# A four-layer graph network kernel whose engine loops are written out

## What is computed

```python
h = jnp.maximum(_layernorm(x), 0.0)
x = x + L0(h)   # typed projections k, q, v; a = <k[src] W, q[dst]> per head; softmax over the
                # edges of a target; sum of v[src] W * attn into dst; projection, norm, FiLM
h = jnp.maximum(_layernorm(x), 0.0)
x = x + L1(h)   # segment_sum of (h * in_degree**-0.5)[src] into dst, * out_degree**-0.5
h = jnp.maximum(_layernorm(x), 0.0)
x = x + L2(h)   # gates = sigmoid(h[src] W_src + h[dst] W_dst + edge_attr W_edge);
                # segment_sum(h[src] W_msg * gates) / segment_sum(gates) + h W_root + b + h
h = jnp.maximum(_layernorm(x), 0.0)
x = x + L3(h)   # gelu(layer_norm(mean of h[src] over the edges of dst @ W_l + b_l + h @ W_r))
```

## Time and profile before

| | us |
|---|---|
| median of 3 runs | 5004.62 |
| lowest, highest | 5002.63, 5007.93 |
| span of the profiled execution | 5005.4 |
| POOL busy | 3394.4 (68%) |
| DVE busy | 3080.3 (62%) |
| PE busy | 3026.9 (60%) |
| ACT busy | 1509.9 (30%) |

### The profile page before, as it was taken

How to read it: one execution, slowest core, us unless ns; L and a number is a source line. 1 busy time by engine, 2 the same in 40 slices (tenths; PEclk the granted TensorE clock), 3 DMA queues, 4 the chain that set the end, 5 groups by cost and what they waited for, 6 DMA issues and landing times.

```text
span 5005.4 us, 77541 instructions
## 1 busy us (share of the span) xinstructions
PE 3026.9 (60%) x15687; PEld 2538.2 (51%) x15688; DVE 3080.3 (62%) x8200; ACT 1509.9 (30%) x2868; POOL 3394.4 (68%) x3564
## 2 busy tenths in 40 slices
PE   6655556555562444455555999999995444444443
PEld 4445555555562444444444777777774344444443
DVE  6567777777777666645453777777775444444443
ACT  2223333333221000011112666666663122222222
POOL 2567777777403777777774777777774777777775
PEclk9667777777775555567676999999998555555555
DMA  3467777788712222222225667767775222222224
GB/s 93 129 184 233 231 225 230 229 227 232 182 35 55 53 52 52 53 63 65 66 65 88 188 187 187 187 187 184 189 187 97 56 56 56 56 56 56 56 56 41
DMA packets 533908, 616.11 MB, mean 123 GB/s; under 512 B 95419, under 2 KB 418043, under 8 KB 533724
## 3 DMA queue, kind: packets, MB, share of 16 engines
q0 software_dynamic: 142256, 349.44, 27.5%
q1 hardware_dynamic: 391468, 264.70, 19.7%
HBM read 529.54 MB, written 84.25 MB: 123 GB/s over the span
## 4 chain that ended last, share of the span: by engine, by line
POOL 44%; issue 20%; DMA 15%; DVE 9%; PE 7%; DVEq 2%; ACT 2%; SPq 1%; POOLq 0%; ACTq 0%
POOL G L708 44%; DMA G<-tab,SRC 10%; DMA mvd<-G 3%; DVE ACCR L1426 3%; PE PB L515 2%; PE PSA L919 1%; PE PB L1106 1%; DVEq L667 1%; PE PB L508 1%; DVE ACCR L1915 1%; DMA MV<-mvd 1%; SPq L791 1%; DVE FLG L1897 1%; ACT PB L1272 0%; ACT L1143 0%
## 5 line engine op out<-in xcount | busy, mean ns | idle before, releaser
L708 POOL DMA_INDIRECT G<-tab,SRC x3520 | 3355.8, 953 | 1378.5 <-issue 1045.4
L1426 DVE TENSOR_TENSOR ACCR<-ACCR,PSA 128x128 f32 (+2 forms) x3536 | 1128.7, 319 | 740.2 <-PE PSA L919 379.9
L919 PE MATMUL PSA<-G,S 128*128 128x128 f32 x3520 | 855.8, 419 | 1159.3 <-DMA G<-tab,SRC 963.9
L919 PEld LDWEIGHTS PSA<-G,S 128*128 128x128 f32 x3520 | 734.7, 309 | 1269.4 <-DVE ACCR L1426 688.8
L1409 DVE TENSOR_TENSOR S<-PB,REL 128x512 f32<-128x512 f32 x884 | 606.5, 686 | 38.6 <-DVE MASK L1478 12.9
L1044 PE MATMUL PB<-QTR,ST 128*128 x1792 | 347.4, 355 | 308.0 <-ACT ST L1235 166.8
L1044 PEld LDWEIGHTS PB<-QTR,ST 128*128 128x128 f32 x1792 | 306.0, 257 | 344.5 <-issue 343.7
L919 PE MATMUL PSA<-FLG,S 128*128 128x256 f32 x1760 | 422.5, 383 | 4.1 <-DVE FLG L1897 3.8
L919 PEld LDWEIGHTS PSA<-FLG,S 128*128 128x128 f32 x1760 | 337.3, 192 | 150.7 <-issue 88.8
L919 PE MATMUL PSA<-SCR,S 128*128 128x137 f32 x1792 | 335.1, 345 | 16.8 <-DVE ACCR L1426 16.7
L919 PEld LDWEIGHTS PSA<-SCR,S 128*128 128x128 f32 x1792 | 311.0, 251 | 21.5 <-DVE SCR L1806 21.5
(11 more groups left out here) (321 smaller groups left out, 3700.5 us busy)
## 6 DMA issues: line engine op xcount, KB each, us to landing
mvd<-G SPq DMA_DIRECT2D x224, 256.0 KB
MV<-mvd SPq DMA_DIRECT2D x224, 256.0 KB
G<-tab,SRC POOLq DMA_INDIRECT x3520, 2.5
SCR<-in_ea_t SPq DMA_DIRECT2D x880, 64.0 KB
S<-relt SPq DMA_DIRECT2D x224, 128.0 KB, 5.1
SCR<-reld SPq DMA_DIRECT2D x220, 128.0 KB
tab<-SCR SPq DMA_DIRECT2D x57, 128.0 KB, 1.8
tab<-G SPq DMA_DIRECT2D x50, 128.0 KB, 1.7
```

The source lines that it names most:

```text
L708: nc.gpsimd.indirect_dma_start(out=rows[:, slot, j, :], out_offset=None, in_=table, in_offset=bass.IndirectOffsetOnAxis(ap=SRC[:, k:k + 1] ...
L919: last = nc.tensor.matmul((PSA if banks is None else banks)[:, par, j, 0:width], S[:, slot, j, :], rhs(j), start=True, stop=True)
L1426: v_.tensor_tensor(rows, rows, banks[:, par, j, 0:width], ALU.add).then_inc(s["rows_added"], 1)
```

## The change

Every `Fori` of the four helpers, of `sp_mixed` and of `sp_results` becomes a Python loop over the same range. The same functions are called with the same indices in the same order, but as numbers: the work instructions, their operands and their semaphores stay, wait values and addresses become constants, and the register arithmetic and branches are gone. Values that come from memory (which block a tile belongs to) are still loaded into registers (`TENSOR_LOAD` at L667 and L675). GpSimd's program is not changed. Two tests in the code change their outcome with the index being a number: `plan(b)` is called for every block, and does nothing above 19; and a wait on a value of zero or less is left out.

```diff
@@ steps
-            if sz.iters > lead + 1:
-                with eng.Fori(lead, sz.iters - 1) as i:
-                    for u in range(UNROLL):
-                        fn(i, u)
+            for i in range(lead, sz.iters - 1):
+                for u in range(UNROLL):
+                    fn(i, u)
@@ layer0_steps
-                with eng.Fori(i, j) as r:
+                for r in range(i, j):
@@ pairs
-            if n > lead + tail:
-                with eng.Fori(lead, n - tail) as i:
-                    for r in range(2):
-                        fn(i * 2 + r, r)
+            for b in range(2 * lead, NS - 2 * tail):
+                fn(b, b % 2)
@@ early_steps
-            with eng.Fori(2, calm) as i:
+            for i in range(2, calm):
...
-            with eng.Fori(first, sz.iters - 1) as i:
+            for i in range(first, sz.iters - 1):
@@ sp_mixed
-            with sp.Fori(1, TURNS_ALL // 2) as k:
-                for r in range(2):
-                    store(k * 2 + r, r)
+            for t in range(2, TURNS_ALL // 2 * 2):
+                store(t, t % 2)
@@ sp_results
-            with sp.Fori(1, TURNS_ALL) as t:
+            for t in range(1, TURNS_ALL):
```

## The result

| | us |
|---|---|
| before, median of 7 runs (range) | 5002.97 (4999.73 to 5007.93) |
| after, median of 7 runs (range) | 4987.85 (4984.73 to 4991.92) |
| ratio, 95% interval | 0.9972 (0.9961 to 0.9982) |
| span of the profiled execution, before and after | 5005.4, 4986.0 |

The change makes the kernel 0.28% faster, 14 us by the ratio, with an interval from 9 to 20. The profiled executions differ by 19.4 us, which is more than the ratio says: that of before was the slowest of its seven.

What follows compares the result with a forecast made beforehand. GpSimd's gathers were taken to bound the edge stages, leaving the second projection's loop: 12.6 + 0.4 + 0.3 = 13.3 us off the 5,004.62 us median gives 4,991.3 us, range 4,987 to 4,997 (4,984 to 5,003 with rival 1 and packets).

Steps and rivals of the forecast that it cites:

- What bounds the kernel: Edge stages: GpSimd's gathers set the rate, 4,457.7 of 5,005.4 us; other engines' edits gain only from GpSimd's waits or between stretches.
- The projection, 12.6 us: Projection behind the scores, 1,440 to 1,509 us: 21 intervals of 2.70 us become 2.10, saving 12.6 us.
- TensorE could do 1.02, VectorE's part comes to 1.05: Second projection, per block: VectorE still late next at 1.05 us, where TensorE's nine matmuls need 1.02.
- The bound of 13.9 us: Second projection: the most to be had if TensorE alone sets the pace, 21 x (2.70 - 2.04).
- Ends of 0.4 and 0.3 us: Entry of the first projection's loop saves some 0.4 us; SyncE's loop of stores at the end 0.3 us.
- Inside the stages 0: Edge stages: no gain from their loops, hidden behind gathers; longer programs also cost 0, at most 10 us.
- The sum: Whole kernel: 12.6 + 0.4 + 0.3 = 13.3 us off the median of 5,004.62, giving 4,991.3 us, 0.27% faster.
- Rival 1: Second projection: only loop control goes, about 0.33 us a turn, 7.7 us with the ends, 4,996.9 us; chance 0.11.
- Rival 2: Scores stage gives back 7 us of short waits and some 3 of gather time, 4,981 us; chance 0.08.
- Rival 3: Gathers: 190 more instruction packets delay them by 0.15 us each, costing 28 us, 5,020 us; chance 0.08.
- Rival 4: Second projection: TensorE's clock stays at 0.50, 30 us more, 5,034 us; chance 0.03.
- The rule on the taken branch: Old loops: a skill's rule that far taken branches stall would speak for more than 12.6 us; no row showed it.

Runs made afterwards that it cites:

- e2: The whole change against the kernel before, except that the projections' helper `pairs` keeps its loop; ratio 1.0002, median 4999.61 us.
- e3: The kernel before with the projections' helper `pairs` written out on VectorE alone; ratio 0.9975, two blocks 2.20 us.
- e4: The kernel before with `pairs` written out on TensorE, ScalarE and SyncE but not on VectorE; ratio 0.9993, two blocks 2.62 us.
- e1: The kernel before with only the projections' helper `pairs` written out, all other loops kept; ratio 0.9971, two blocks 2.12 us.
- e7: The changed kernel with VectorE's residual add of the second projection one block later; ratio 0.9964 against before, two blocks 2.00 us.
- e9: The changed kernel with an empty two-turn loop on VectorE before each even block of the second projection; ratio 0.9993 against before, two blocks 2.38 us.
- e5: The kernel before with four blocks a turn in the second projection's loop, register waits kept; ratio 0.9985, two blocks 2.27 or 2.70 us.
- e6: The kernel before with each pair of blocks in `pairs` a loop of one turn; ratio 0.9970, two blocks 2.12 us.
- e8: The changed kernel with 40 more ScalarE semaphore increments per step in turns 2 to 25 of the last edge stage; ratio 0.9983 against before.

## Why the prediction was right, and where not

**What bounds the kernel: right.** The stages stayed at GpSimd's rate. e2 is the proof: all edge loops gone, ratio 1.0002 (0.9993 to 1.0011).

**The projection, 12.6 us: right in place, engine and about in size.** A turn went from 2.70 to 2.12 us, where I had 2.10: 21 x 0.58 = 12.2. e3 and e4 confirm that VectorE was the engine, but for 0.08 of the 0.58, which belong to TensorE's loop; e1 and e2 show that no other loop counts. The mean seam is 228.1 us in the three kernels with all loops in the pairs (229.1, 227.5, 227.8) and 215.9 in those five above: 12.2 us.

**"TensorE could do 1.02, VectorE's part comes to 1.05": wrong in its reading.** The 1.05 of the last two blocks was no engine's own time. In before VectorE does a block in 0.92 us where it waits for nothing, from its L555 at 1503.07 to this one:

```profile
1503.99 0.55 DVE L555 TENSOR_TENSOR G<-ACCR 128x384 f32 x1
```

And 1.05 is every second interval of TensorE, in the loop and behind it, whatever the other one is: 1.65 over a jump, 1.22 from 1504.81 to 1506.03 in the earlier trace rows, which was not counted. Two blocks of that end take 2.27 us; that twice 1.05 came so close to the 2.12 of the change was in part luck. VectorE's work and TensorE's work both fit in 1.00 (e7). The two waited for each other over the order of VectorE's instructions, and one block of delay for the add removes it. The bound of 13.9 us, from 1.02, was therefore too low: 21 x (2.70 - 2.00) = 14.7. The 0.113 us for one more matmul came from two group rows whose ends are modelled.

**Ends of 0.4 and 0.3 us: not to be seen one by one.** The first gather comes at 173.9 us in the mean of the five kernels that loop over the first projection on VectorE (174.7, 173.2, 174.1, 173.2, 174.3) and at 173.1 in the mean of the seven that have it written out on all engines. That is of the order of 0.4 and proves little, since e3, with VectorE's loop gone, has 175.0. SyncE's loop at the end shows no gain: the time from the last gather to the end is 38.6 to 40.2 with it (eight profiles), 38.0 to 40.0 without (six).

**Inside the stages 0: at most a small term missing.** I took 0 for the longer programs and had 10 us as the bound. The three stages are some 2 us longer with them; that it is the packets isn't shown.

**The sum.** 12.2 + 0.4 - 2 is 10.6, and the timed gain is 14 (9 to 20) and 13 (8 to 18). Both hold the 13.3 of the forecast and the 10.6 of the repaired sum. The time came out 3.4 us below the 4,991.3, and about half of that is the anchor: the median of three runs that I subtracted from, 5,004.62, became 5,002.97 with seven. I also compared the span with the median, 0.8 us apart, where the execution of that span had itself taken 5,007.93, or 3.3 over the median.

**Rivals.** Rival 1 (only loop control goes, 2.70 to 2.37) fell: the turn is 2.12. But its mechanism is half of the truth, since the bare jump with its control is 0.26 of the 0.58 (e9). Its price of 0.33 lies between that and the 0.35 (0.61 - 0.26) by which the copies come later behind the add, and what it denied, the cost of register waits, is there too (e5). Rival 2 (the scores stage gives back) fell: with its loops 1,162.4 us in the mean of eight (1,159.2 to 1,167.5), without 1,161.7 in the mean of six. Rival 3 (packets) fell: 0.01 us a packet at the most, where 0.07 would decide. Rival 4 (clock): 1.00 in the blocks, as before.

**The rule on the taken branch.** The Trainium skill (Runtime: NRT & Kernel Launch, "Instruction fetch mechanics") has a taken branch stall when its target is outside the blocks held. The jump of e9 lands a few instructions back, and 0.14 us pass behind it; in before the jump over two blocks' instructions does the same (the branch starts at 1502.55, and the next register instruction at 1502.74). The length of the jump makes no difference here, and no longer pause shows; which blocks were held, the traces don't say.

## What to carry to other kernels

Write out the one loop whose engines hand blocks to each other on the path between two stages, and leave the others: here 44 blocks gave the whole gain, and the rest only lengthened the program. Whether a loop is such a one is seen in the timeline of the engine that waits: a gap at every back edge, and none or a small one between. And when the last blocks of a loop are taken for what straight code would do, look whether the time between them is an engine's own or a wait passed to and fro; in the second case a change in the order of one engine's instructions can earn something too, here 0.06 us a block.

## What the runs showed of the hardware

- A taken branch on VectorE costs about 0.2 us from its start to the next instruction (1481.38 to 1481.58 in e9), a branch not taken 0.10 to the next work instruction, and nothing on the path when work covers it (e6: 22 of them, same 2.12 us).
- A bare jump on VectorE with its control makes two blocks 0.26 us longer, where VectorE's work before it covers the rest (e9: 0.51 us from L573 to L555 in place of 0.26).
- Of the six register waits that VectorE has in two blocks, only those count that no work covers: the one ahead of L573, 0.14 us, without any jump (e5), and the one ahead of L555, with the rest of its register work 0.10, when it comes right behind a jump (before against e9).
- A packet of instructions (128 instructions: 7,680 in 60 packets in e8) costs a GpSimd-bound stage under 0.01 us, 1,099.2 us against 1,098.7 to 1,099.3 in four kernels without them.
- TensorE's transposes start 0.12 us behind the copies when it has just jumped back, and 0.04 otherwise (e5, e4).
- TensorE holds 1.00 us a block of nine matmuls, without a gap (e7).
